# Two causal attentions of an eight-stage fp32 kernel: loads of later head groups issued from ScalarE one a unit, and a third weight buffer with a second accumulator

## The chip, the core and the metric

The kernel runs on one core of one Trainium2 chip. The core has TensorE (PE, matmuls; PEld in the profile is its weight load), VectorE (DVE), ScalarE (ACT), GpSimd (POOL) and SyncE (SP), which work side by side and wait for one another by semaphores. Each engine takes its own instructions in order. The metric is the device time of one execution in microseconds (us).

## What is computed

The reference passes `x`, 2048 rows of 128, through eight residual layers: RWKV, a mixture of experts, rotary attention, the mixture again, full attention, a second expert layer, latent attention, and that expert layer again. The change touches the two causal attentions:

```
q = apply_rope(q); k = apply_rope(k)                 # rotary: 16 heads of 8
scores = einsum('bhqd,bhkd->bhqk', q, k) / sqrt(8)
attn = softmax(where(causal, scores, -inf))
x = x + einsum('bhqk,bhkd->bhqd', attn, v) @ W_out.T

k = k_lat @ wk_up; v = v_lat @ wv_up                 # latent: 8 heads, 2 groups, rank 32
probs = softmax(where(causal, q @ k * 128**-0.5, min))
x = x + (probs @ v) @ wo
```

All is fp32 to the outside. Scores are made from operands that are split into three bf16 parts and stacked in the contraction rows.

## The kernel before

The whole program is one list of stages. `CausalHeads` (L1084) is used twice. Heads are worked four at a time, a "quad": four quads in the rotary stage, two in the latent one. A quad's 2048 queries are cut into four chunks `c` of 512 columns; a chunk has `4*(c+1)` key tiles, and one key tile of one chunk for four heads is a **unit**. The rotary stage goes through the chunks quad by quad (units 0 to 159, chunk (g,c) of quad g; quads begin at units 0, 40, 80 and 120), the latent stage alternates its quads (80 units; chunks begin at units 0, 4, 8, 16, 24, 36, 48 and 64).

In a unit PE makes the scores of two head pairs (`pe_scores`), ACT turns each pair into exponentials in a buffer `PT` (L1433), and one unit later PE multiplies them into bank 4 (`pe_weighted`, L1391). `PT` has two buffers, so the exponentials of unit u wait until unit u-2 has been used. At a chunk's end ACT copies bank 4 into `O` (L1442).

Between these, `make_plan` (L1197) lays out "ring items" in three PSUM banks that PE fills and DVE empties in order:

- `max`: part of the row maxima of a coming chunk. PE L1320 makes scores, DVE L1555 reduces them. After a chunk's last one DVE runs five small operations (L1564 to L1571) that make the negated maximum in three bf16 parts
- `turn`: PE transposes those parts (L1331), DVE copies them (L1577), and SP sends them by four DMAs into rows of `Q` (`max_row_dmas`, L1702)
- `sum`: the softmax denominators, broadcast; DVE then makes `On`, the normalised output (L1590 rotary, L1587 latent)
- `out`: PE projects `On` (L1349), DVE adds it to `X` (L1596)

The **rotary** stage gets its denominators as a ninth output row: SP moves them out of `O` into `sums` (L1736), DVE inverts them (L1533), SP moves them back (L1739), and PE broadcasts them (L1344). These two "relays" stand in the plan two and four units behind the end of the chunk, `sum` and `out` six and seven. DVE waits for the relay's DMA in its own order. Quad 0's stacked operands `Q` and `K` are loaded chunk by chunk (`load_early`). Those of quads 1 to 3 are loaded by SP in `sync`, with eight DMAs (`load_stacks`, L1626; three for `Q`, five for `K`, 2.3 MB in all), right behind the maximum rows of chunk (g,1). `Q` and `K` have two slots, so for g of 1 or more SP waits first until all units of quad g-1 are done. In SP's list this stands just ahead of the relay `sums` of quad g-1's last chunk.

The **latent** stage adds its exponentials up over the key tiles: for every unit POOL adds three heads and DVE one head of `PT` to `acc` (`add_weights`; L1475 copies at a chunk's first unit, L1477 adds at the others). There is one `acc`. The first unit of a chunk therefore waits, on both engines, until PE has read the last chunk's sums (L1340, one item in the tail of the second unit behind the chunk's end). `out` follows one unit behind `sum`. `PT` lies in the memory of `w0` and `w0b`, `acc` in `pbelow`, which are free by then; the trace shows these names.

POOL's other work is `Perturb.gpsimd` (L577 to L597), a search in 31 rounds for the second expert layer, that runs beside the rotary and the following stages.

Of the kernel before, what the change touches and what calls it, by code (L numbers as in the profile page):

```python
# [1083 lines left out]
class CausalHeads(Stage):  # L1084
# [76 lines left out]
    def alloc(self, ctx):  # L1161
# [5 lines left out]
        self.acc = self.homes[2] if self.summed else None  # L1167
# [10 lines left out]
        if self.homes:  # L1178
            self.PT = self.homes[0:2]
        else:  # L1180
            with ExitStack() as c:
                pt = self.k.sb(self.name + "_PT", [P, 2, 4, CH], F32, c)
                self.PT = [pt[:, b, :, :] for b in range(2)]
        with ExitStack() as c:
            self.x = self.k.sb(self.name + "_x", [P, ns, CH], F32, c)
            if self.rotate:
                self.y = self.k.sb(self.name + "_y", [P, CH], F32, c)
                self.tab = self.k.sb(self.name + "_tab", [P, 2, T], F32, c)
# [10 lines left out]
    def make_plan(self):  # L1199
# [31 lines left out]
        for n, (g, c) in enumerate(self.order):  # L1231
            end = self.starts[n + 1] - 1
            if self.summed:
                steps[end + 2].append(("sum", g, c))
                steps[end + 3].append(("out", g, c))
            else:
                relays.append((end + 2, "sums", g, c))
                relays.append((end + 4, "reciprocals", g, c))
                steps[end + 6].append(("sum", g, c))
                steps[end + 7].append(("out", g, c))  # L1240
# [66 lines left out]
    def pe_item(self, pe, item, bank):  # L1307
# [25 lines left out]
        if kind == "sum":  # L1333
            _, g, c = item
            n = self.chunk(g, c)
            if self.summed:
                pe.wait_ge(self.added[0], self.first_unit(n + 1))
                pe.wait_ge(self.added[1], self.first_unit(n + 1))
                for j in range(4):
                    ins = pe.matmul(k.PS[32 * j:32 * j + 32, bank, :], k.ones_col, self.acc[:, j, :],  # L1340
                                    start=True, stop=True)
# [37 lines left out]
    def pe_weighted(self, pe, u):  # L1379
# [9 lines left out]
        for j in range(4):  # L1389
            v = self.V[:, kj, (4 * g + j) if self.vheads > 4 else g, :]  # L1390
            ins = pe.matmul(k.PS[32 * j:32 * j + self.vcols, 4, q0:CH], v, self.PT[u % 2][:, j, q0:CH],  # L1391
# [4 lines left out]
    def scalar(self, s):  # L1396
# [26 lines left out]
        for u in range(total + 1):  # L1423
            if u < total:
                _, _, _, q0 = self.unit(u)
                if u >= 2:
                    s.wait_ge(self.weighted, u - 1)
                    if self.summed:
                        s.wait_ge(self.added[0], u - 1)
                        s.wait_ge(self.added[1], u - 1)  # L1430
                for p in range(2):
                    s.wait_ge(self.scores[p], u + 1)
                    s.activation(self.PT[u % 2][:, 2 * p:2 * p + 2, q0:CH], k.PS[:, 2 * p:2 * p + 2, q0:CH],  # L1433
                                 ACT.Exp, scale=self.scale).then_inc(self.exps[p], 1)
            if u:
# [26 lines left out]
    def add_weights(self, eng, u, who, heads):  # L1462
# [3 lines left out]
        if kj == 0 and n:  # L1466
            b, uses = self.ring_bank(self.ring_items().index(("sum",) + self.order[n - 1]))
# [5 lines left out]
        new, acc = self.PT[u % 2][:, heads, q0:CH], self.acc[:, heads, q0:CH]  # L1473
# [139 lines left out]
    def load_stacks(self, sp, g, cols, planes, done):  # L1613

        d = P // self.heads
        for operand, heads, (src, h), blocks in ((self.Q, 4, self.q_source(g), self.blocks[0]),
                                                 (self.K, self.kheads, self.k_source(g), self.blocks[1])):
            for block in blocks:
                for m, row, first, parts in self.parts_of(*block):
                    if m not in planes:  # L1620
                        continue
# [83 lines left out]
    def sync(self, sp):  # L1705
# [12 lines left out]
        for u, item in self.plan:  # L1718
            if item[0] == "turn":
# [7 lines left out]
                if c == 1 and self.early < len(self.order) and g + 1 < self.NQ:  # L1727
                    if g:
                        sp.wait_ge(self.weighted, self.starts[self.index[g, 0]])
                    self.load_stacks(sp, g + 1, slice(0, T), range(self.NP), self.stacked[(g + 1) % 2])  # L1730
# [259 lines left out]
def build(nc, d, upto=8, start=0):  # L1990
    with ExitStack() as ctx:
# [79 lines left out]
        def latent_attention():  # L2071
# [8 lines left out]
                            homes=[k.w0[:, :, :].rearrange("p (j e) h -> p j (e h)", j=4),  # L2080
                                   k.w0b[:, :, :, :].rearrange("p (j e) m d -> p j (e m d)", j=4),
                                   perturb.below[:, :, :, :].rearrange("p w s n -> p (w s) n")])
# [66 lines left out]
```

## Time and profile before

| | us |
|---|---|
| median of 3 runs (1888.04 to 1889.11) | 1888.36 |
| the profiled execution | 1890.95 |
| its span, from first to last instruction | 1888.7 |
| PE busy in the span | 1593.5 (84%) |
| DVE busy | 1159.4 (61%) |
| POOL busy | 818.2 (43%) |
| ACT busy | 787.2 (42%) |

The profiled execution took 2.6 us more than the median run, and 2.25 us of it lie outside its span. Times in the rows are us from the span's start. In a timeline row the first two numbers are start and duration, and the square brackets give how long the engine was idle before and what ended the idle time. Operations of one kind in a row are merged (x8). SPq and ACTq are DMA issues.

### The profile page before, as it was taken

The page shows a single profiled execution, that of the slowest core. Times are in us where ns is not written, and L with a number is a line of the kernel's source. Part 1 is how long each engine was busy: PE and PEld are TensorE (multiplying, and loading weights), DVE is VectorE, ACT ScalarE, POOL GpSimd, SP SyncE. Part 2 cuts the span into 40 slices and gives each one's busy share as a digit, 9 for nine tenths or more (in the row PEclk, how much of TensorE's full clock was granted, in tenths as well). Part 3 has the DMA queues.
Part 4 walks back from the last instruction along what each step waited for, and adds up shares of the span by engine and source line. Part 5 has one row for each costly group of instructions (what it writes and reads, how often), then busy time and mean ns, then how long its engine had stood idle before and what let it go on. Part 6 is the DMA issues. An engine that isn't in the chain of part 4 may idle for free. (4 is left out here: it accounts for less than half of the span.)

```text
span 1888.7 us, 25915 instructions
## 1 busy us (share of the span) xinstructions
PE 1593.5 (84%) x8863; PEld 804.5 (43%) x8863; DVE 1159.4 (61%) x2315; ACT 787.2 (42%) x1031; POOL 818.2 (43%) x987
## 2 busy tenths in 40 slices
PE   4766699769996996899979978998978889898779
PEld 2222466423332332333246655775644333333256
DVE  5887633499785785788343343334268888876551
ACT  2222233353553563565743333444442333444533
POOL 1224655455545463645455456000003456667900
PEclk8788699877998998999979999998988898988979
DMA  4000000143003002000000000000033000000000
GB/s 142 1 0 0 1 1 0 45 117 52 1 4 50 1 16 38 2 2 2 2 1 1 0 0 0 0 0 1 1 120 108 22 22 1 1 1 1 1 1 23
DMA packets 39122, 36.88 MB, mean 20 GB/s; under 512 B 10190, under 2 KB 36271, under 8 KB 38898
## 3 DMA queue, kind: packets, MB, share of 16 engines
q1 hardware_dynamic: 38842, 35.56, 7.9%
q8 instruction: 61, 1.00, 0.2%
q14 instruction: 35, 0.29, 0.1%
q10 hardware_dynamic: 120, 0.02, 0.0%
q0 software_dynamic: 64, 0.00, 0.0%
HBM read 26.10 MB, written 8.91 MB: 19 GB/s over the span
## 5 line engine op out<-in xcount | busy, mean ns | idle before, releaser
L1555 DVE TENSOR_REDUCE sb_rope_mp<-PS 128x1 f32<-128x512 f32 (+3 forms) x560 | 345.5, 669 | 70.3 <-PE PS L1324 32.9
L1433 ACT ACTIVATE sb_rope_PT<-PS 128x1024 f32<-128x1024 f32 (+3 forms) x320 | 273.3, 895 | 220.1 <-PE PS L1372 119.3
L1320 PE MATMUL PS<-sb_rope_K,sb_rope_Q 96*128 96x512 bf16 (+3 forms) x640 | 214.7, 375 | 43.7 <-DVE sb_rope_mp L1555 33.0
L1000 DVE SCALAR_TENSOR_TENSOR sb_X<-PS,sb_gates,sb_X 128x128 f32 (+1 forms) x320 | 90.1, 345 | 238.8 <-PE PS L948 238.6
L581 POOL TENSOR_SCALAR sb_pbelow<-sb_pa,sb_ptrial 128x512 f32<-128x512 f32 x124 | 196.2, 1593 | 6.4
L1555 DVE TENSOR_REDUCE sb_latent_mp<-PS 128x1 f32<-128x512 f32 (+2 forms) x280 | 174.9, 667 | 29.5 <-PE PS L1320 22.5
L588 POOL TENSOR_TENSOR sb_pbelow<-sb_pbelow 128x1024 f32<-128x1024 f32 (+1 forms) x248 | 181.8, 733 | 19.6
L936 PE MATMUL PS<-sb_HT,sb_w 128*128 (+1 forms) x384 | 182.5, 612 | 3.6 <-DVE sb_seed L519 1.9
L1372 PE MATMUL PS<-sb_rope_Q,sb_rope_K 99*128 99x512 bf16 (+3 forms) x640 | 181.5, 355 | 1.6 <-ACT sb_rope_PT L1433 0.9
L1372 PE MATMUL PS<-sb_latent_Q,sb_latent_K 96*128 96x512 bf16 (+7 forms) x640 | 160.0, 371 | 8.2 <-ACT sb_w L1433 4.7
L977 ACT ACTIVATE sb_moe_hidden<-PS,sb_vec 128x512 f32<-128x512 f32 x128 | 87.8, 687 | 159.7 <-PE PS L936 155.4
L1391 PE MATMUL PS<-sb_rope_PT,sb_rope_V 128*9 128x512 f32 (+3 forms) x1280 | 150.7, 543 | 0.1
L1320 PEld LDWEIGHTS PS<-sb_rope_K,sb_rope_Q 96*128 96x128 bf16 x640 | 60.0, 100 | 200.2 <-issue 88.1
L1475 POOL COPY sb_pbelow<-sb_w 128x1536 f32<-128x1536 f32 x8 | 13.2, 1655 | 293.7 <-ACT sb_w L1433 241.3
L1477 POOL TENSOR_TENSOR sb_pbelow<-sb_pbelow,sb_w0b 128x1536 f32<-128x1536 f32 (+2 forms) x40 | 118.0, 2949 | 45.9 <-ACT sb_w0b L1433 44.1
L948 PE MATMUL PS<-sb_w0b,sb_moe_hidden 128*128 128x128 f32 x1024 | 131.3, 281 | 0.0
L1320 PE MATMUL PS<-sb_latent_K,sb_latent_Q 96*128 96x512 bf16 (+3 forms) x320 | 105.6, 377 | 25.1 <-DVE sb_latent_rec L1585 11.9
L948 PEld LDWEIGHTS PS<-sb_w0b,sb_moe_hidden 128*128 128x128 f32 x1024 | 119.1, 191 | 14.5 <-issue 14.5
L1433 ACT ACTIVATE sb_w<-PS 128x1024 f32<-128x1024 f32 (+1 forms) x80 | 73.5, 938 | 109.6 <-PE PS L1376 40.4
L1477 POOL TENSOR_TENSOR sb_pbelow<-sb_pbelow,sb_w 128x1536 f32<-128x1536 f32 (+1 forms) x32 | 105.8, 3307 | 24.0 <-ACT sb_w L1433 22.2
L1433 ACT ACTIVATE sb_w0b<-PS 128x1024 f32<-128x1024 f32 (+2 forms) x80 | 67.3, 853 | 112.4 <-PE PS L1372 53.0
L594 POOL TENSOR_TENSOR sb_ptot<-sb_ptot,sb_prank 128x8 f32<-128x8 f32 x31 | 6.5, 211 | 225.2 <-issue 225.2
(296 smaller groups left out, 2552.7 us busy)
## 6 DMA issues: line engine op xcount, KB each, us to landing
sb_latent_Q<-latent_parts SPq DMA_DIRECT2D x48, 128.0 KB, 2.7
sb_rope_Q<-rope_parts SPq DMA_DIRECT2D x9, 384.0 KB
rope_parts<-sb_rope_parts SPq DMA_DIRECT2D x24, 128.0 KB, 2.4
latent_parts<-sb_latent_parts SPq DMA_DIRECT2D x12, 256.0 KB, 2.6
sb_rope_tab<-in_rotation SPq DMA_DIRECT2D x1, 2048.0 KB, 8.5
sb_rope_K<-rope_parts SPq DMA_DIRECT2D x6, 256.0 KB
latent_parts<-sb_latent_parts SPq DMA_DIRECT2D x12, 128.0 KB, 2.5
sb_latent_K<-latent_parts SPq DMA_DIRECT2D x48, 32.0 KB, 2.2
```

Source lines behind the costliest of these rows:

```text
L581: ch.mark(g.tensor_scalar(self.below[:, w, s, :], self.a[:, w, :], tr[:, 2 * w + s:2 * w + s + 1], None, ALU.is_lt))
L588: ch(g.tensor_tensor(bl[:, :, 0:n], bl[:, :, 0:n], bl[:, :, n:2 * n], ALU.add))
L936: pe.matmul(k.bank(b), self.w1(e, m), x, start=True, stop=True).then_inc(self.hid[b], 1)
L948: ins = pe.matmul(k.PS[:, 4 + b, i * P:(i + 1) * P], self.g[:, b, m, i * P:(i + 1) * P], self.w2(e, m), start=False, stop=(m == M - 1), sk ...
L977: s.activation(self.g[:, e % 2, m, :], k.bank(b), self.func, bias=self.b1(e, m)) \
L1000: ins = v.scalar_tensor_tensor(xi, k.PS[:, 4 + b:5 + b, i * P:(i + 1) * P], gate, xi, ALU.mult, ALU.add)
L1320: ins = pe.matmul(k.PS[:, bank, at:at + w], self.Q[0:self.rows, g % 2, j, 0, q0:q0 + P], self.K[0:self.rows, g % 2, j % self.kheads, 0, kc ...
L1372: ins = pe.matmul(k.PS[:, j, q0:CH], self.K[0:r, g % 2, j % self.kheads, m, kj * P:(kj + 1) * P], self.Q[0:r, g % 2, j, m, c * CH + q0:(c ...
L1391: ins = pe.matmul(k.PS[32 * j:32 * j + self.vcols, 4, q0:CH], v, self.PT[u % 2][:, j, q0:CH], start=(kj == 0), stop=(kj == last))
L1433: s.activation(self.PT[u % 2][:, 2 * p:2 * p + 2, q0:CH], k.PS[:, 2 * p:2 * p + 2, q0:CH], ACT.Exp, scale=self.scale).then_inc(self.exps[p ...
L1477: eng.tensor_tensor(acc, acc, new, ALU.add).then_inc(self.added[who], 1)
L1555: v.tensor_reduce(self.mp[:, n % 2, kc, heads[0]:heads[-1] + 1, i], k.PS[:, bank, 0:len(heads) * w].rearrange("p (h k) -> p h k", h=len(he ...
```

## The change

1. **Rotary, loads.** SP no longer loads the stacks of quads 1 to 3. ACT does it, from its own DMA queue, in the eight units of chunk (g,1): behind the exponentials of each unit it issues one of the eight DMAs (`load_quad`). At the first of them it waits for the units of quad g-1 or, for g=0, for the written constants and the stored parts.
2. **Latent, accumulators.** There are two `acc`, by parity of the chunk, the second in the memory of `H`. The first unit of a chunk waits for the sums of the chunk before the last, not of the last.
3. **Latent, buffers.** `PT` has a third buffer, in the memory of `HT` from column 1 on. The exponentials of unit u wait for unit u-3.
4. **Latent, output.** `out` stands two units behind `sum` in the plan, not one.

```diff
             if self.summed:
                 steps[end + 2].append(("sum", g, c))
-                steps[end + 3].append(("out", g, c))
+                steps[end + 4].append(("out", g, c))
...
-                if u >= 2:
-                    s.wait_ge(self.weighted, u - 1)
+                if u >= self.B:
+                    s.wait_ge(self.weighted, u - self.B + 1)
                     if self.summed:
-                        s.wait_ge(self.added[0], u - 1)
-                        s.wait_ge(self.added[1], u - 1)
+                        s.wait_ge(self.added[0], u - self.B + 1)
+                        s.wait_ge(self.added[1], u - self.B + 1)
                 for p in range(2):
                     s.wait_ge(self.scores[p], u + 1)
-                    s.activation(self.PT[u % 2][:, 2 * p:2 * p + 2, q0:CH], k.PS[:, 2 * p:2 * p + 2, q0:CH],
+                    s.activation(self.PT[u % self.B][:, 2 * p:2 * p + 2, q0:CH], k.PS[:, 2 * p:2 * p + 2, q0:CH],
                                  ACT.Exp, scale=self.scale).then_inc(self.exps[p], 1)
+                self.load_quad(s, u)
...
-        if kj == 0 and n:
-            b, uses = self.ring_bank(self.ring_items().index(("sum",) + self.order[n - 1]))
+        if kj == 0 and n >= 2:
+            b, uses = self.ring_bank(self.ring_items().index(("sum",) + self.order[n - 2]))
             eng.wait_ge(self.ring_full[b], uses + 1)
...
-        new, acc = self.PT[u % 2][:, heads, q0:CH], self.acc[:, heads, q0:CH]
+        new, acc = self.PT[u % self.B][:, heads, q0:CH], self.acc[n % 2][:, heads, q0:CH]
...
+    def load_quad(self, s, u):
+
+        g, c, kj, _ = self.unit(u)
+        if self.early == len(self.order) or g + 1 == self.NQ or c != 1:
+            return
+        if kj == 0:
+            if g:
+                s.wait_ge(self.weighted, self.starts[self.index[g, 0]])
+            else:
+                s.wait_ge(self.constants, self.constants0 + self.n_constants)
+                s.wait_ge(self.stored_lo, self.lo_done(NC - 1))
+                s.wait_ge(self.stored_hi, self.hi_done(NC - 1))
+        if kj < self.stack_dmas:
+            self.load_stacks(s, g + 1, slice(0, T), range(self.NP), self.stacked[(g + 1) % 2], [kj])
...
-                if c == 1 and self.early < len(self.order) and g + 1 < self.NQ:
-                    if g:
-                        sp.wait_ge(self.weighted, self.starts[self.index[g, 0]])
-                    self.load_stacks(sp, g + 1, slice(0, T), range(self.NP), self.stacked[(g + 1) % 2])
...
-                            homes=[k.w0[:, :, :].rearrange("p (j e) h -> p j (e h)", j=4),
-                                   k.w0b[:, :, :, :].rearrange("p (j e) m d -> p j (e m d)", j=4),
-                                   perturb.below[:, :, :, :].rearrange("p w s n -> p (w s) n")])
+                            homes=[[k.w0[:, :, :].rearrange("p (j e) h -> p j (e h)", j=4),
+                                    k.w0b[:, :, :, :].rearrange("p (j e) m d -> p j (e m d)", j=4),
+                                    k.HT[:, 1:1 + T].rearrange("p (j t) -> p j t", j=4)],
+                                   [perturb.below[:, :, :, :].rearrange("p w s n -> p (w s) n"),
+                                    k.H[:, :, :].rearrange("p (j n) d -> p j (n d)", j=4)]])
```

## Rows read from the trace of the kernel before

**Rows 1.** The page's first part: busy time of each engine, share, instructions.

```profile
PE 1593.5 (84%) x8863; PEld 804.5 (43%) x8863; DVE 1159.4 (61%) x2315; ACT 787.2 (42%) x1031; POOL 818.2 (43%) x987
```

**Rows 2.** Windows: span; busy PE, PEld, DVE, ACT, POOL; granted clock, DMA share, GB/s.

```profile
443.00:957.00 514.00, 452.20 (x3128) 173.19 (x3127) 363.35 (x647) 281.87 (x337) 264.91 (x441) 0.94 0.10 14
...
1430.00:1802.00 372.00, 317.10 (x1911) 124.43 (x1909) 292.55 (x405) 145.95 (x169) 237.00 (x80) 0.90 0.04 12
```

**Rows 3.** Timeline around quad 2's load, from 566 to 589 us.

```profile
566.16 2.18 SPq L1626 DMA_DIRECT2D sb_rope_K<-rope_parts  x5
...
568.38 0.60 SPq L1736 DMA_DIRECT2D sb_rope_sums<-sb_rope_O  x1
...
587.64 0.25 DVE L1533 RECIPROCAL sb_rope_rec<-sb_rope_sums 128x16 f32<-128x16 f32 x1 [15.34 <-DMA sb_rope_sums<-sb_rope_O]
...
588.50 0.61 PE L1320 MATMUL PS<-sb_rope_K,sb_rope_Q 96*128 96x512 bf16 x1 [14.90 <-DVE sb_rope_mp L1555]
```

**Rows 4.** Timelines around quad 3's load.

```profile
706.93 0.60 SPq L1736 DMA_DIRECT2D sb_rope_sums<-sb_rope_O  x1
...
726.56 0.25 DVE L1533 RECIPROCAL sb_rope_rec<-sb_rope_sums 128x16 f32<-128x16 f32 x1 [15.53 <-DMA sb_rope_sums<-sb_rope_O]
```

**Rows 5.** Windows just behind the two loads; columns as in rows 2.

```profile
588.00:604.00 16.00, 14.67 (x72) 4.79 (x73) 11.96 (x24) 6.31 (x7) 2.10 (x8) 0.77 0.01 2
...
726.50:742.00 15.50, 13.30 (x70) 4.53 (x70) 13.63 (x24) 6.30 (x7) 12.39 (x19) 0.83 0.01 2
```

**Rows 6.** Timelines at the rotary stage's start: what DMA issues take on either queue.

```profile
416.57 3.67 ACTq L1702 DMA_DIRECT2D sb_rope_Q<-sb_rope_negT  x4
...
433.82 3.16 SPq L1702 DMA_DIRECT2D sb_rope_Q<-sb_rope_negT  x4
```

**Rows 7.** SP's timeline: the relay's two DMAs, chunks (0,1) and (3,3).

```profile
481.81 0.58 SPq L1736 DMA_DIRECT2D sb_rope_sums<-sb_rope_O  x1
489.37 0.54 SPq L1739 DMA_DIRECT2D sb_rope_O<-sb_rope_rec  x1
...
952.81 0.55 SPq L1736 DMA_DIRECT2D sb_rope_sums<-sb_rope_O  x1
954.94 0.53 SPq L1739 DMA_DIRECT2D sb_rope_O<-sb_rope_rec  x1
```

**Rows 8.** Waits in the rotary stage: who for whom, us in total, times, longest.

```profile
ACT sb_rope_PT L1433 <- PE PS L1372: 119.3, 94, 6.6
...
PE PS L1331 <- DVE sb_rope_negp L1571: 22.5, 12, 4.0
```

**Rows 9.** Timeline of one chunk border of the latent stage (unit 16).

```profile
1511.45 1.06 PE L1340 MATMUL PS<-sb_pbelow,sb_cst 128*32 128x512 f32 x8
...
1512.59 0.43 DVE L1475 COPY sb_pbelow<-sb_w 128x512 f32<-128x512 f32 x1 [2.01 <-PE PS L1340]
...
1513.86 3.35 DVE L1585 RECIPROCAL sb_latent_rec<-PS 128x512 f32<-128x512 f32 x1
...
1517.26 0.61 PE L1320 MATMUL PS<-sb_latent_K,sb_latent_Q 96*128 96x512 bf16 x1 [2.00 <-DVE sb_latent_rec L1585]
...
1517.92 3.77 POOL L1477 TENSOR_TENSOR sb_pbelow<-sb_pbelow,sb_w 128x1536 f32<-128x1536 f32 x1
...
1519.98 2.27 DVE L1477 TENSOR_TENSOR sb_pbelow<-sb_pbelow,sb_w0b 128x512 f32<-128x512 f32 x1
```

**Rows 10.** Sum over windows of 15 to 21 us at the six borders before the last.

```profile
sum 113.00, PE 96.30 PEld 37.16 DVE 97.74 ACT 33.49 POOL 59.61; mean PE 16.05 PEld 6.19 DVE 16.29 ACT 5.58 POOL 9.94
```

**Rows 11.** POOL's timeline at the last border (unit 64).

```profile
1735.16 3.42 POOL L1477 TENSOR_TENSOR sb_pbelow<-sb_pbelow,sb_w0b 128x1536 f32<-128x1536 f32 x1 [0.65 <-ACT sb_w0b L1433]
1744.25 3.44 POOL L1477 TENSOR_TENSOR sb_pbelow<-sb_pbelow,sb_w 128x1536 f32<-128x1536 f32 x1 [5.67 <-ACT sb_w L1433]
1748.47 3.94 POOL L1477 TENSOR_TENSOR sb_pbelow<-sb_pbelow,sb_w0b 128x1536 f32<-128x1536 f32 x1 [0.78 <-ACT sb_w0b L1433]
```

**Rows 12.** Window of the rest of the last chunk; columns as in rows 2.

```profile
1748.00:1793.00 45.00, 33.87 (x220) 10.87 (x216) 26.62 (x14) 22.39 (x27) 43.59 (x13) 0.97 0.00 1
```

More of the change, by code:

```diff
@@ L1166, in alloc @@
         self.V = sb("V", [P, NT, self.vheads, self.vcols])
-        self.acc = self.homes[2] if self.summed else None
+        self.acc = self.homes[1] if self.homes else None
         self.mp = sb("mp", [P, 2, NC, 4, TPC])
@@ L1178, in alloc @@
         if self.homes:
-            self.PT = self.homes[0:2]
+            self.PT = self.homes[0]
+            self.B = len(self.PT)
         else:
@@ L1183, in alloc @@
                 self.PT = [pt[:, b, :, :] for b in range(2)]
+                self.B = 2
         with ExitStack() as c:
@@ L1339, in pe_item @@
                 for j in range(4):
-                    ins = pe.matmul(k.PS[32 * j:32 * j + 32, bank, :], k.ones_col, self.acc[:, j, :],
+                    ins = pe.matmul(k.PS[32 * j:32 * j + 32, bank, :], k.ones_col, self.acc[n % 2][:, j, :],
                                     start=True, stop=True)
@@ L1390, in pe_weighted @@
             v = self.V[:, kj, (4 * g + j) if self.vheads > 4 else g, :]
-            ins = pe.matmul(k.PS[32 * j:32 * j + self.vcols, 4, q0:CH], v, self.PT[u % 2][:, j, q0:CH],
+            ins = pe.matmul(k.PS[32 * j:32 * j + self.vcols, 4, q0:CH], v, self.PT[u % self.B][:, j, q0:CH],
                             start=(kj == 0), stop=(kj == last))
@@ L1611, in parts_of, with load_stacks @@
         return [(m, row + 32 * p, first + p, 1) for p in range(parts)]
-    def load_stacks(self, sp, g, cols, planes, done):
-        d = P // self.heads
+    def load_quad(self, s, u):
[11 more added lines that the diff above has]
+            self.load_stacks(s, g + 1, slice(0, T), range(self.NP), self.stacked[(g + 1) % 2], [kj])
+    def load_stacks(self, sp, g, cols, planes, done, only=None):
+        d, made = P // self.heads, 0
         for operand, heads, (src, h), blocks in ((self.Q, 4, self.q_source(g), self.blocks[0]),
@@ L1619, in load_stacks @@
                 for m, row, first, parts in self.parts_of(*block):
-                    if m not in planes:
+                    made += 1
+                    if m not in planes or (only and made - 1 not in only):
                         continue
```

## The prediction

> **What bounds the kernel now.** I read the page's first part, then windows by stage, then in the two stages that the change touches the waits, and at the longest waits the timeline. The page says that PE is busy 84% of the span and no other engine over 61% [rows 1]. That is a mean over eight stages, so it doesn't tell what this change is worth. The windows do: the rotary units last 514 us with PE busy 452, the latent ones 372 us with PE busy 317 and a mean granted clock of 0.90 [rows 2]. PE bounds both stages, except where something stops it, and those places are what an edit off PE can give back. Outside these two stages nothing changes.
>
> In the rotary stage the timeline shows one kind of large stop. SP has issued quad 2's eight loads, and the relay `sums` of chunk (0,3) is issued right behind them at 568.38. DVE, in order, reaches the reciprocal and sits idle for 15.34 us until that small transfer lands. The ring then stands full, PE is idle 14.90 us, and ACT with it [rows 3]. At quad 3's load the same follows: issued at 706.93, DVE idle 15.53 us [rows 4]. Quad 1's load comes ahead of the first unit and costs no such stop. In the latent stage each chunk border has its pattern: DVE idle 2.01 us for PE's sums, then a reciprocal of 3.35 us, which holds a ring bank, then PE idle 2.00 us for it [rows 9]. In the last chunk POOL is the bound instead: busy 43.59 of 45 us [rows 12].
>
> **Rotary, what is removed.** The relay no longer stands behind the loads. With an empty queue the relay goes from issue through reciprocal to the second issue in 2.13 us [rows 7]; at 566 or so DVE would have its sums at about 568.5, and it came for them at 587.64 - 15.34 = 572.3 [rows 3]. So both stops go entirely: 15.34 + 15.53 = 30.9 us, and since all engines stood still in them, nothing else fills the place. Behind each stop PE ran at a mean clock of 0.77 for 16 us and 0.83 for 15.5 us [rows 5], so up to 3.7 + 2.6 = 6.3 us more. I take 4, since the second window holds another short stop of its own.
>
> **Rotary, what is added.** ACT issues 24 DMAs. On SP the five `K` loads take 2.18 us, 0.44 each [rows 3]; four issues of maximum rows took 3.67 us on ACT and 3.16 on SP [rows 6], so a load's issue on ACT is about 0.44 x 3.67 / 3.16 = 0.51 us, 24 of them 12. They stand behind a unit's exponentials, ahead of the wait for the next unit's scores. ACT waits there: 94 times and 119.3 us in the stage [rows 8], 1.27 each. That covers 0.51, so I take 0; if the cover is gone it is 12. What is queued behind the issue is the next unit's exponentials and, at a chunk's end, the copy of bank 4; PE waits for both. The new waits at the first unit are for things long done (units before the last one, stores before the first): 0. Not below 0, since ACT issued none before.
>
> The loads are wanted at the next quad's first `max` items, units 23, 62 and 102 by the plan, and the last is issued in unit 11, 51 or 91. So eleven units lie between, over 30 us against 19.3 us for a whole load (568.38 to 587.64 [rows 3]): 0. But now the load moves while units run, and three relays (0,0), (1,0) and (2,0) fall in it. No row shows a small transfer beside another queue's load. Lower end: as with an empty queue, 2.1 us. Upper end: as behind everything, 19.3. The relay has 489.37 - 481.81 = 7.6 us until the reciprocal in the usual rhythm [rows 7]. One load in eight is 19.3 / 8 = 2.4 us; even behind two of them the relay lands in 2.1 + 4.8 = 6.9 us, so I take 0, and keep (19.3 - 7.6) x 3 = 35 us as the far end.
>
> The row shows only that one queue is served in order. The Trainium skill (DMA: Bandwidth & Descriptors, Issuing engines are not separate DMA queues) says that DMAs from any engine run on the same 16 DMA engines and interleave, and that another issuing engine only saves the sequencer's time to issue. That speaks against this part: by it alone the gain would be little more than the 3.3 us of issue per load; by the row it is 15.4 a load. The spread over eight units is what decides, and the rule has nothing against that.
>
> A shift of the rotary units also moves them against POOL's search. PE waited 22.5 us in 12 waits for DVE's small operations at `turn` [rows 8], some of which are stretched while POOL works. I take 0 and +-6 us.
>
> Rotary in sum: 30.9 + 4 = 35 us faster, from 20 to 43.
>
> **Latent, the last border.** POOL ends the add of unit 65 at 1738.6 and begins the next at 1744.25, idle 5.67 us for ACT, then 0.78 [rows 11]. The exponentials of unit 66 waited for DVE's copy of unit 64, which stands behind reciprocal and `On` in DVE's order, and the second pair waited for PE, which stood at `out` for `On`. With three buffers the copy is not asked for, and `out` comes a unit later. Then POOL goes on at once, and since it bounds what follows [rows 12], the stage ends 5.67 + 0.78 = 6.4 us sooner; I take 6.
>
> **Latent, the six others.** DVE's copy no longer waits for the sums (2.01 us), so the items behind it are done before they come and the reciprocal begins at the sums' end, 1512.5, not 1513.86: 1.3 us. PE's wait of 2.00 behind it shrinks by that, the exponentials no longer wait for POOL's copy, and PE's slow matmuls behind its idle time should go in part. The six windows have 113.0 - 96.3 = 16.7 us of PE idle, 2.8 a border [rows 10]. I take 2.5 a border with the clock, 15 us. Lower end 0: a later reciprocal's `On` may meet a POOL add. Upper end 5 a border: all idle time and as much again for the clock. Moving `out` costs no work; `H` and `HT` as homes change neither counts nor sizes, and only the chunk that begins at unit 8 has its first copy from `HT`. Latent in sum: 21 us, from 3 to 36.
>
> The rows show what limits it: DVE's add at 1519.98 took 2.27 us while POOL's ran from 1517.92 to 1521.69 [rows 9]. The Trainium skill (SBUF — State Buffer, SBUF: two separate sides) says that DVE and GpSimd share a port pair by an exclusive lock for a whole instruction. By that rule, the trace agrees: the add ended 0.56 us behind POOL's. By it a POOL that starts sooner is one that DVE meets more often, and the rule's own result is the slower rival below.
>
> **Rivals.**
> (A) *The relay crawls beside the loads.* For it: 2.3 MB are on their way in those units. Against: small transfer, 7.6 us of room. It costs up to 35 us of the 56: 1867. The stops would be three, at chunks (g,0).
> (B) *Latent gives only its last border or nothing*, because DVE's operations land behind POOL's adds: the gain is 35 + 0 to 6, 1847 to 1853. For it: the 2.27 us above. Against: POOL's adds are as many as before.
> (C) *Slower: DVE becomes the latent stage's bound.* With ACT free to run ahead, POOL starts each add before DVE comes to its own, and DVE waits for the whole of it, 3.42 us [rows 11], in each of the 64 units before the last chunk, 219 us. DVE has 372 - 292.6 = 79 us idle [rows 2], so 140 remain, less the 35 of the rotary part: 105 slower, 1993. It decides when the mean add grows by (79 + 35) / 64 = 1.8 us. Against: PE's own pace hardly lets ACT run ahead where `max` items fill the ring.
> (D) *ACT's issues have no cover and the relays crawl in part*: rotary gains 20, 1847.
>
> **How the numbers follow.** Forecast 35 + 21 = 56 us. In the profiled execution: span 1888.7 - 56 = 1832.7, with 2.25 outside 1835; the median run is 2.6 below, 1832.4. Say 1832. Chances: forecast with its own bounds (1814 to 1846) 0.68; (B) 0.15; (D) 0.07; (A) 0.05; (C) 0.03; no change 0.02. The range holds the forecast's spread, (B) and (D): 1815 to 1855. A difference of 0.2% (3.8 us) is about what a measurement of this kernel can tell from none; faster by more 0.95, within 0.02, slower 0.03.
>
> **What would show it.** Right: no DVE wait at L1533 of over 2 us near the quads' starts, the rotary units near 479 us instead of 514 in the windows; eight ACTq issues L1626 a quad; DVE's copy L1475 without a wait for L1340; POOL's copy under 1 us behind ACT's exponentials; POOL without a gap over 1 us behind unit 65; ACT no longer released by L1475. Wrong: L1533 released by DMA at chunks (0,0), (1,0), (2,0); ACT idle time released by PE falling by less than the issues; DVE adds L1477 of over 2 us in most units; latent units still 372 us.

## The result, and the profile after

The changed kernel takes 1856.18 us (median of 3 runs, 1855.55 to 1856.32) where the kernel before took 1888.36: a ratio of 0.983, 95% interval 0.981 to 0.985. It is faster, by 32 us and not by the 56 forecast, and 1856 lies 1.2 us above the range. The profiled execution took 1856.32 us, its span 1854.2.

The table splits it. "Rotary units" runs from the first exponential to the issue of the last chunk's `sums` relay, "latent units" from the first exponential to the end of POOL's last add; the four parts and the constant rest make up the span.

| us | before | after | gained | forecast |
|---|---|---|---|---|
| up to the first rotary exponential | 443.7 | 439.1 | 4.5 | 0 |
| rotary units | 509.2 | 479.1 | 30.1 | 35 |
| moe2, full attention, ffn1, latent projections | 478.0 | 482.2 | -4.2 | 0 |
| latent units | 362.2 | 358.0 | 4.2 | 21 |

First the windows of the changed kernel, with the columns of [rows 2]: the rotary and the latent stage, and POOL's last chunk, which answers to [rows 12].

```profile
439.00:918.00 479.00, 452.63 (x3125) 174.41 (x3123) 360.62 (x645) 280.11 (x336) 249.36 (x415) 0.97 0.08 17
1400.00:1767.00 367.00, 310.50 (x1910) 123.03 (x1908) 310.75 (x405) 146.57 (x169) 220.96 (x80) 0.90 0.04 12
1715.90:1758.50 42.60, 32.53 (x213) 10.63 (x212) 39.08 (x13) 22.59 (x26) 41.59 (x13) 0.93 0.00 1
```

In the rotary stage PE is busy as long as before (452.6 against 452.2 us), though the units are 30 us shorter (the window of [rows 2] is 4.8 us longer than its units, this one is not). The mean granted clock rose from 0.94 to 0.97, but PE's busy time didn't fall. In the latent stage POOL is busy 16 us less and DVE 18 us more, with as many instructions on each: DVE's operations have become longer. In the last chunk POOL is the bound as before.

The timelines of SP, ACT and DVE in the changed kernel around quad 2's load, which answer to [rows 3]:

```profile
573.08 0.30 ACTq L1645 DMA_DIRECT2D sb_rope_Q<-rope_parts  x1
573.40 1.02 ACT L1435 ACTIVATE sb_rope_PT<-PS 128x1024 f32<-128x1024 f32 x1
574.93 0.55 SPq L1751 DMA_DIRECT2D sb_rope_sums<-sb_rope_O  x1
...
585.56 0.24 DVE L1536 RECIPROCAL sb_rope_rec<-sb_rope_sums 128x16 f32<-128x16 f32 x1
585.82 0.59 SPq L1754 DMA_DIRECT2D sb_rope_O<-sb_rope_rec  x1
```

The relay goes between two loads, and the reciprocal has no wait in brackets. Before it sat idle for 15.34 us. ACT's issue takes 0.30 us and ends before the next exponential; up to 800 us, behind the last load, no wait of DVE for this transfer is left (30.9 us before, in two). The waits for the stage's last two relays stay, 11.8 and 20.1 us. They are in every trace (9 to 12 and 20 us) and have nothing to do with the loads: these relays are issued late, and are read 2 us behind their issue.

One border of the latent stage, which answers to [rows 9], from the timeline of the changed kernel:

```profile
1487.81 3.36 DVE L1588 RECIPROCAL sb_latent_rec<-PS 128x512 f32<-128x512 f32 x1 [0.23 <-PE PS L1342]
1491.04 3.42 POOL L1480 TENSOR_TENSOR sb_H<-sb_H,sb_w 128x1536 f32<-128x1536 f32 x1 [1.92 <-ACT sb_w L1435]
1491.20 3.80 DVE L1590 TENSOR_TENSOR sb_latent_On<-sb_latent_O,sb_latent_rec 128x512 f32<-128x512 f32 x1
1494.92 1.14 DVE L1558 TENSOR_REDUCE sb_latent_mp<-PS 128x1 f32<-128x384 f32 x2
1495.53 0.61 PE L1322 MATMUL PS<-sb_latent_K,sb_latent_Q 96*128 96x512 bf16 x1 [3.91 <-DVE sb_latent_mp L1558]
1497.96 1.02 ACT L1435 ACTIVATE sb_w0b<-PS 128x1024 f32<-128x1024 f32 x1 [7.09 <-PE PS L1374]
1501.62 3.62 POOL L1480 TENSOR_TENSOR sb_H<-sb_H,sb_w0b 128x1536 f32<-128x1536 f32 x1 [7.17 <-ACT sb_w0b L1435]
```

The waits that the edit was to remove are gone: no 2.01 us for the sums, no 2.00 behind the reciprocal. In their place stands `On`. It begins 0.16 us behind POOL's add and ends 0.54 us behind it. The maxima queue behind it, PE finds its ring full for 3.91 us, ACT waits 7.09 us for PE and POOL 7.17 us for ACT. The same comes at five borders. `On` over the stage (shortest, median, longest in ns, from the view of that line):

```profile
L1590 DVE TENSOR_TENSOR sb_latent_On<-sb_latent_O,sb_latent_rec x8: 691/3290/3803, 1425.1 to 1763.9; 128x512 f32<-128x512 f32 x8
```

In the kernel before, `On` came when a POOL add was nearly over. The timelines of POOL and DVE at the border of [rows 9]:

```profile
1514.41 3.43 POOL L1477 TENSOR_TENSOR sb_pbelow<-sb_pbelow,sb_w0b 128x1536 f32<-128x1536 f32 x1
1517.24 1.15 DVE L1587 TENSOR_TENSOR sb_latent_On<-sb_latent_O,sb_latent_rec 128x512 f32<-128x512 f32 x1
```

It began 0.60 us before that add's end and ended 0.55 us behind it, and POOL's next add, begun meanwhile at 1517.92, took 3.77 us instead of 3.42. Its median over the stage was 0.89 us.

### The profile page after: what moved, and what is told of

It is laid out like the page before. It is cut to its first block, busy times and chain, and to the rows that moved or that the text cites. A ratio compares the mean times of both kernels' runs of the same rounds, so it can differ in the third digit from the quotient of the medians.

```text
span 1854.2 us, 25913 instructions
## 1 busy us (share of the span) xinstructions
PE 1591.2 (86%) x8863; PEld 808.5 (44%) x8863; DVE 1173.7 (63%) x2315; ACT 787.9 (42%) x1031; POOL 802.9 (43%) x987
## 4 chain that ended last, share of the span: by engine, by line
PE 67%; DVE 15%; issue 3%; ACT 3%; POOL 2%; DMA 0%; DVEq 0%; POOLq 0%; SPq 0%; ACTq 0%
PE PS L1374 11%; PE PS L948 10%; PE PS L1322 10%; PE PS L936 9%; PE PS L1393 9%; PE PS L1822 3%; PE PS L1840 3%; DVE sb_rope_mp L1558 3%; POOL sb_H L1480 2%; DVE sb_latent_mp L1558 2%; DVE sb_latent_rec L1588 1%; PE PS L1834 1%; PE PS L941 1%; PE PS L1032 1%; PE PS L1351 1%
## 5 line engine op out<-in xcount | busy, mean ns | idle before, releaser
L936 PEld LDWEIGHTS PS<-sb_HT,sb_w 128*128 128x128 f32 x384 | 71.0, 199 | 71.7 <-issue 68.2
L1478 POOL COPY sb_pbelow<-sb_w 128x1536 f32<-128x1536 f32 x3 | 4.4, 1464 | 225.9 <-ACT sb_w L1435 219.3
L836 POOL TENSOR_TENSOR sb_rw_kvj<-sb_rw_k,sb_rw_vj 128x512 f32<-128x512 f32 x32 | 43.9, 1378 | 131.2 <-ACT sb_rw_vj L819 92.1
L1374 PEld LDWEIGHTS PS<-sb_latent_Q,sb_latent_K 99*128 99x128 bf16 (+1 forms) x640 | 59.0, 103 | 82.5 <-issue 22.3
L593 POOL PARTITION_ALL_REDUCE sb_ptot<-sb_pcnt x31 | 13.2, 427 | 186.3 <-issue 186.3
```

What stands on the lines that cost most here:

```text
L936: pe.matmul(k.bank(b), self.w1(e, m), x, start=True, stop=True).then_inc(self.hid[b], 1)
L1374: ins = pe.matmul(k.PS[:, j, q0:CH], self.K[0:r, g % 2, j % self.kheads, m, kj * P:(kj + 1) * P], self.Q[0:r, g % 2, j, m, c * CH + q0:(c ...
```

## The experiments

Three chips carried them. There one kernel's runs spread by 0.5 to 1%, so each time is read against the kernel before on the same chip (medians 1891.1, 1893.9, 1887.0 and 1887.2 us in the four groups), and most verdicts rest on the length of the two stages in the trace. The latent units of the changed kernel were 358.0 to 358.1 us in all five traces with that code, whatever the chip.

| kernel | rotary units | latent units | median us | ratio to before, 95% |
|---|---|---|---|---|
| before | 509.2 | 362.2 | 1888.4 | |
| changed | 479.1 | 358.0 | 1856.2 | 0.981 to 0.985 |
| changed, once more | 478.0 | 358.1 | 1854.2 | 0.976 to 0.988 |
| rotary part alone | 472.5 | 367.6 | 1862.3 | 0.980 to 0.989 |
| latent part alone | 506.4 | 358.1 | 1881.9 | 0.993 to 0.999 |
| burst from ACT | 509.0 | 358.0 | 1884.6 | 0.994 to 0.999 |
| spread from SP | 478.5 | 358.0 | 1852.9 | 0.976 to 0.985 |
| POOL held | 465.8 | 350.6 | 1849.4 | 0.974 to 0.983 |
| reciprocal in PSUM | 479.2 | 342.3 | 1832.4 | 0.964 to 0.971 |
| same, one accumulator | 471.7 | 359.5 | 1858.2 | 0.981 to 0.991 |
| same, latent part of before | 480.7 | 368.4 | 1864.4 | 0.982 to 0.992 |
| `HT` from element 0 | 465.3 | 362.5 | 1854.6, one run | |
| `w0` 8, `w0b` 64 bytes on | 476.0 | 359.4 | 1856.2, one run | |
| `w0` 4, `w0b` 36 bytes on | 468.4 | 347.2 | 1844.1 | 0.973 to 0.981 |
| reciprocal in PSUM and 4, 36 on | 475.3 | 329.1 | 1830.4 | 0.966 to 0.976 |
| the same, once more | 463.8 | 329.2 | 1825.9 | 0.962 to 0.974 |
| and `neg` in PSUM | 460.8 | 324.7 | 1813.7 | 0.955 to 0.966 |

**The two halves.** Each half with the other as before.

> The rotary part alone (quads' stacks loaded from ScalarE's queue, one transfer a unit; latent stage as in the kernel before). Theory: the rotary part is worth the two removed stops, 30 us between first exponential and last sums of the changed kernel's trace (509.2 against 479.1 us), and nothing is given back later: 1888.4 - 30 = 1858 us, 1854 to 1862. Rival: the clock behind the missing stops and POOL's search, which now meets other stages, take part of it back: 1866 or more, and then the latent part must be worth over 10.

> The latent part alone (two accumulators, three PT buffers, out two units behind sum; rotary loads as before). Theory: of the 21 us forecast only the last border's 6.4 us arrive, since at the five borders before it DVE's On multiply now begins just behind POOL's add and waits for its end (2.6 to 3.1 us each): latent units 362 to 358 us, so 1888.4 - 4 = 1884 us, 1881 to 1887. Rival: latent gained its 15 to 21 us and the rotary part gave less than the units' 30: 1867 to 1873.

Both came within their ranges but for 0.3 us (1862.3, 1881.9). The ranges were counted from 1888.4, though, and the kernel before took 1891.1 on this chip: read as gains, the latent half gave 9 us where 1 to 7 was expected, of which its latent units show 4.1. The rotary half is worth 29 us by the medians, the latent half 9, with an interval of 2 to 13. What neither text said: with its code unchanged, the latent stage took 367.6 us in the first, not 362.2. In the chunk that begins at unit 48, which took 73.2 us and not 64.4, three of DVE's own adds had fallen into step behind POOL's. The timelines of POOL and DVE in that kernel:

```profile
1647.41 3.42 POOL L1480 TENSOR_TENSOR sb_pbelow<-sb_pbelow,sb_w 128x1536 f32<-128x1536 f32 x1 [2.83 <-ACT sb_w L1435]
1647.45 3.93 DVE L1480 TENSOR_TENSOR sb_pbelow<-sb_pbelow,sb_w0b 128x512 f32<-128x512 f32 x1
```

An add of 0.67 us on its own takes 3.93 when it begins 0.04 us behind POOL's. So even the old stage isn't fixed to better than 5 us. Which engine comes first by some hundredths seems to decide it; what brings that about was not tried.

**Is it the queue or the spreading?** The first kernel issues all eight loads from ACT at once, the second one a unit from SP.

```diff
-        if kj < self.stack_dmas:
-            self.load_stacks(s, g + 1, slice(0, T), range(self.NP), self.stacked[(g + 1) % 2], [kj])
+        if kj == 0:
+            self.load_stacks(s, g + 1, slice(0, T), range(self.NP), self.stacked[(g + 1) % 2])
```

> The changed kernel, but ScalarE issues all eight loads of a quad at once in chunk 1's first unit, not one a unit: another queue, no spreading. Theory (order of one queue made the stops): the relay, on SP's own queue, still goes in 2 to 3 us beside the eight loads, DVE's waits for the sums stay under 3 us, time as the changed kernel, 1856 (1853 to 1860). Rival (the transfers share the DMA engines whatever the queue, so spreading was what helped): the relay crawls for most of the load's 19 us, DVE waits 5 to 15 us in two or three chunks, 1866 to 1886.

In SP's function, where `load_quad` now waits for unit u's exponentials ahead of its load:

```diff
         for u, item in self.plan:
-            if item[0] == "turn":
+            if item == "weighted":
+                self.load_quad(sp, u)
+            elif item[0] == "turn":
```

> The changed kernel, but SP issues the loads, one a unit behind the unit's exponentials, in its order with the relays: spreading, same queue. Theory (order of one queue, by quantity): the relay stands behind at most one load of 2.4 us, for which it has 7.6 us of room, so no stop comes back: 1856 (1853 to 1860). Rival (a relay behind any load on its queue is stopped for long): stops of over 5 us at the first chunk of quads 0 to 2, 1866 or more.

The burst brought the stops back, 1884.6 us: its relay, on SP's own and empty queue, was issued at 455.84, and its reciprocal came 19 us later; at the two other loads it was 19.9. Its timelines of SP and DVE, then DVE's waits from 440 to 800 us (total, times, longest):

```profile
455.84 0.63 SPq L1751 DMA_DIRECT2D sb_rope_sums<-sb_rope_O  x1
...
474.89 0.25 DVE L1536 RECIPROCAL sb_rope_rec<-sb_rope_sums 128x16 f32<-128x16 f32 x1 [11.14 <-DMA sb_rope_sums<-sb_rope_O]
```

```profile
DVE sb_rope_rec L1536 <- DMA sb_rope_sums<-sb_rope_O: 33.3, 3, 11.9
```

Spread over units from SP, the loads cost nothing, 1852.9 us, rotary units 478.5 (from ACT 479.1 and 478.0). So the spreading is the whole gain, and the change of engine is worth nothing here. The Trainium skill (DMA: Bandwidth & Descriptors, Issuing engines are not separate DMA queues) says that transfers share the 16 DMA engines whoever issues them. By that rule, the burst's trace agrees, with its 11.14 us.

**Is `On` long because of POOL?** First POOL's add of each chunk's third unit is made to wait for the `On` of the chunk before:

```diff
+        if who == 0 and kj == 2 and n:
+            eng.wait_ge(self.normed, n)
```

> The changed kernel, and POOL's add of each chunk's third unit waits for the On of the chunk before. Theory: On (3.29 to 3.80 us at five borders, 0.69 alone) lasts long only because it begins 0.04 to 0.18 us behind POOL's add; with POOL held for under 1 us it takes 0.7, PE's stops of 3 to 4 us behind it go, and POOL comes no later for its next exponentials, for which it waits 6.5 to 7.6 us now: (3.80 + 3.80 + 3.41 + 3.29 + 3.29) - 5 x 0.69 = 14 us faster, 1842, between 1836 and 1848. Rival: On's length is its own (its operands, its place), or PE is late for another reason: 1856 to 1858, and PE's stops stay.

`On` took 0.69 us at all five borders, so its length was POOL's. The latent units fell by 7.4 us, not by 14; the median, 1849.4, is just outside. The timeline shows where the other half went:

```profile
1478.35 0.69 DVE L1592 TENSOR_TENSOR sb_latent_On<-sb_latent_O,sb_latent_rec 128x512 f32<-128x512 f32 x1
1479.50 3.42 POOL L1482 TENSOR_TENSOR sb_H<-sb_H,sb_w 128x1536 f32<-128x1536 f32 x1 [3.23 <-DVE sb_latent_On L1592]
1480.03 3.44 DVE L1482 TENSOR_TENSOR sb_H<-sb_H,sb_HT 128x512 f32<-128x512 f32 x1
1484.13 0.61 PE L1322 MATMUL PS<-sb_latent_K,sb_latent_Q 96*128 96x512 bf16 x1 [3.08 <-DVE sb_latent_mp L1560]
```

The held add starts after `On`, and DVE's own add, next but one in its order, meets it. PE stops for 3.08 us instead of 3.91. That part of my expectation was wrong: I had taken the collision for one of `On` alone, and DVE's adds meet it as well.

Then `On` is given an operand in PSUM, and POOL isn't held:

```diff
-                v.reciprocal(self.rec[:, :], k.bank(bank)).then_inc(free, 1)
-                v.wait_ge(free, uses + 1)
-                v.tensor_tensor(self.On[:, n % 2, :], self.O[:, n % 2, :], self.rec[:, :], ALU.mult) \
+                ch(v.reciprocal(k.bank(bank), k.bank(bank)))
+                v.tensor_tensor(self.On[:, n % 2, :], self.O[:, n % 2, :], k.bank(bank), ALU.mult) \
...
+                v.wait_ge(self.normed, n + 1)
+                v.sem_inc(free, 1)
```

> The changed kernel, and the reciprocal is written in place into its PSUM bank, so that On multiplies SBUF by PSUM; POOL is not held. Theory: what DVE shares with POOL is used only by operations whose operands all lie in SBUF (maxima, which read PSUM, took 0.68 us beside every add); then On takes 0.7 us beside POOL's add and the time is about that of the kernel with POOL held, 1842, 1836 to 1850, the ring bank being held 1 us longer a border. Rival: On waits for POOL's add wherever its second operand lies: then also the bank is held for the whole add, and it is 1856 to 1870.

```profile
1489.24 3.42 POOL L1480 TENSOR_TENSOR sb_H<-sb_H,sb_w 128x1536 f32<-128x1536 f32 x1 [1.92 <-ACT sb_w L1435]
1489.41 0.69 DVE L1589 TENSOR_TENSOR sb_latent_On<-sb_latent_O,PS 128x512 f32<-128x512 f32 x1
1490.24 1.16 DVE L1558 TENSOR_REDUCE sb_latent_mp<-PS 128x1 f32<-128x384 f32 x2
1491.31 1.90 DVE L1480 TENSOR_TENSOR sb_H<-sb_H,sb_HT 128x512 f32<-128x512 f32 x1
1493.87 0.39 PE L1322 MATMUL PS<-sb_latent_K,sb_latent_Q 96*128 96x512 bf16 x1 [1.53 <-DVE sb_latent_mp L1558]
```

`On` begins 0.17 us behind POOL's add, in the very place where it took 3.80, and takes 0.69. DVE's add comes when half of POOL's is over. Latent units 342.3 us, 15.7 less than the changed kernel, and 1832.4 (4 us below the range). The theory holds. The Trainium skill (SBUF — State Buffer, SBUF: two separate sides) says that the exclusive lock is met by a DVE operation with two SBUF inputs, against a GpSimd operation that reads SBUF, or by one in a 2-port performance mode. By that rule, the rows agree: 0.69 with one SBUF input, 3.80 with two.

**What is the latent part worth without the collision?** The in-place reciprocal with the latent stage of before, and with everything of the change but the second accumulator (`self.acc = [self.homes[1][0]] * 2`, and the first copy of a chunk waits for the sums again):

> Rotary part as changed, latent stage as in the kernel before, but with the reciprocal in place in PSUM. It asks what the latent part is worth once On no longer meets POOL. Theory: On was 0.9 to 1.5 us in the old latent stage, 2.7 at the last border, so the in-place form brings it only some 4 us; DVE's and POOL's waits for PE's sums and POOL's 5.7 us at the last border stay: latent units 358 to 364 us, against 342.3 with the latent part, and 1855 to 1862. Rival: the in-place reciprocal is what helped, the latent part is worth nothing: units 342 to 346.

> The kernel with the reciprocal in place, but one accumulator instead of two (three PT buffers and out two units behind sum stay). Theory: the second accumulator is what lets POOL and DVE begin a chunk without waiting for PE's sums; without it the waits of about 2 us a border come back at DVE and POOL, and since ACT has a third buffer they are passed on only in part: latent units 342.3 + 1 to 2 a border, 348 to 357, 1840 to 1848. Rival: the third buffer alone carries it: 342 to 344.

The first gave 368.4 us, so in these traces the latent part is worth 26 us once `On` is out of POOL's way. I had expected 358 to 364; the in-place form alone gains nothing on the old stage (367.6). In both of these traces the chunk of unit 48 has DVE's adds in step behind POOL's (here three of 3.73 to 3.93 us, from 1659.96 to 1672.26). Against 362.2, the old stage without that, the latent part would be worth 20. The second gave 359.5 us, beyond the 357 expected, and 1858.2: the second accumulator carries 17 of it. The wait for the sums is back in its waits:

```profile
POOL sb_pbelow L1478 <- PE PS L1342: 55.6, 7, 11.3
```

**The 2.90 us adds.** In the changed kernel POOL's adds from `HT` took 2.90 us at the least, those from `w0` and `w0b` 3.42. `HT` is used from its element 1. Three kernels move the buffers by a few bytes:

```diff
-                                    k.HT[:, 1:1 + T].rearrange("p (j t) -> p j t", j=4)],
+                                    k.HT[:, 0:T].rearrange("p (j t) -> p j t", j=4)],
```

and, with `w0b` likewise (2 and 8 elements in the second kernel, 1 and 1 in the third):

```diff
-        k.w0 = sb("w0", [P, 8, 256])
+        k.w0 = sb("w0", [P, 1 + 8 * 256])[:, 1:].rearrange("p (e h) -> p e h", e=8)
```

> The changed kernel with the third PT buffer in HT from its element 0, not 1, so 4 bytes lower. POOL's adds with HT took 2.90 us where those with w0 and w0b took 3.42. Theory (the offset of 4 bytes against the accumulator does it): all adds take 3.42 now, and the time is up to 8 us longer, since POOL's adds of the last chunk stand in the path: 1858 to 1864. Rival (the place of HT in SBUF does it): adds with HT stay at 2.90, same time.

> The changed kernel with w0 8 bytes and w0b 32 bytes further on, HT at 4 bytes as before. Theory: what counts is that operand and accumulator differ in the low bits of a pair of 4-byte elements: adds with w0 (8) and w0b (32) take 3.42 us, with HT 2.90. Rival: any distance does it: 2.90 with w0 too, or with both.

> The changed kernel with w0 and w0b laid 4 bytes further on, as HT's columns lie. Theory (the offset of 4 bytes): POOL's adds with all three buffers take 2.90 us; the last chunk, where POOL goes without idle time, has ten adds with w0 or w0b of up to 0.52 us less, 4 us, and DVE waits for shorter adds before: 1849, 1845 to 1853. Rival (place): adds with w0 and w0b stay at 3.42, 1856.

POOL's adds grouped by form (busy, mean ns, idle before), first from element 0 of `HT`, then the second kernel, then the third:

```profile
L1480 POOL TENSOR_TENSOR sb_pbelow<-sb_pbelow,sb_HT 128x1536 f32<-128x1536 f32 x8 | 28.9, 3609 | 14.5 <-ACT sb_HT L1435 14.4
```

```profile
L1480 POOL TENSOR_TENSOR sb_pbelow<-sb_pbelow,sb_w0b 128x1536 f32<-128x1536 f32 x8 | 28.3, 3543 | 14.0 <-ACT sb_w0b L1435 14.0
...
L1480 POOL TENSOR_TENSOR sb_pbelow<-sb_pbelow,sb_w 128x1536 f32<-128x1536 f32 x8 | 24.7, 3092 | 22.0 <-ACT sb_w L1435 22.0
```

```profile
L1480 POOL TENSOR_TENSOR sb_pbelow<-sb_pbelow,sb_w 128x1536 f32<-128x1536 f32 x8 | 24.7, 3090 | 23.0 <-ACT sb_w L1435 23.0
L1480 POOL TENSOR_TENSOR sb_pbelow<-sb_pbelow,sb_w0b 128x1536 f32<-128x1536 f32 x8 | 24.1, 3018 | 10.7 <-ACT sb_w0b L1435 10.7
```

The latent units fell by 10.8 us with both buffers shifted, more than the last chunk's 5, probably since a shorter add also blocks DVE for less; the time, 1844.1 us, is 1 us below the range. From element 0 they rose by 4.5. The time of that kernel stayed at 1854.6: its rotary units were 13.8 us shorter than the changed kernel's, and the stages between 9.3 longer (491.5).

**Both together.**

> The two edits together on the changed kernel: reciprocal in place in PSUM, and w0 and w0b 4 bytes further on. Alone they brought the latent units from 358.0 to 342.3 and to 347.2 us. Theory (both take from the same thing, DVE standing behind POOL's adds, and only the last chunk's ten adds of 0.5 us are the shift's own): latent units 337 us, 335 to 340, and the time 1827, 1820 to 1834. Rival (independent): 342.3 - 10.8 = 331.5 us, 1821. Other rival: a new rhythm of DVE and POOL takes it back, 342 or more.

> The kernel with both edits once more, beside the one with neg in PSUM on the same chip. Expected: latent units 329 us as before, rotary units anywhere from 465 to 481 by where the search falls, 1830.

Latent units 329.1 and 329.2, better than the sum of the parts (331.5) and than I expected; 1830.4 and 1825.9 us.

**Why the rotary units vary.** With the same rotary code (spread loads) they took from 463.8 to 480.7 us. The idea is that the length goes with what meets POOL's search. The four small operations behind a chunk's maxima (`negp`, both operands in SBUF) took, in the sum from 440 to 903 us, 12.2 and 13.3 us where the units were 465.3 and 465.8, and 20.1 to 21.6 where they were 478.0 to 480.7; the other traces lie between, but for 463.8 at 14.9. The last kernel puts `neg` in PSUM:

```diff
-                neg, part = self.neg[:, n % 2, :, :], self.negp[:, n % 2, :, :, :]
+                neg = k.PS[:, bank, 0:4 * TPC].rearrange("p (j i) -> p j i", j=4)
+                part = self.negp[:, n % 2, :, :, :]
...
+                v.wait_ge(self.maxima, n + 1)
+                v.sem_inc(free, 1)
```

The last two lines free the bank, now behind the five operations.

> The kernel with both edits (reciprocal in place, w0 and w0b shifted), and the negated maxima `neg` of each chunk in the PSUM bank of the chunk's last max item instead of SBUF, so that each of the five small operations behind a chunk's maxima has an operand in PSUM. Theory: the rotary units' length (465 to 481 us in ten traces with the same rotary code) goes with how many of these operations meet POOL's search, and an operand in PSUM keeps them out of it: each takes under 0.25 us in the mean (before up to 0.62), PE's wait for negp in the rotary units falls from 15 to 22 us to about 14, rotary units 463 to 468 us; in the latent units the casts of up to 2.9 us go as well, 329 to 322 to 327; in all 1820 to 1826 against 1830. Rival: their length is not POOL's, or the bank held about 1 us longer a chunk costs as much: rotary units stay between 470 and 480, same time.

> The changed kernel itself beside these two. Theory (the latent units have one rhythm, the rotary ones go with the search): latent units 358.0 us again, rotary units from 465 to 481, with DVE's casts behind the maxima long where the units are long; 1850 to 1860.

The casts in the rotary units (busy, mean ns), in the changed kernel run once more and in this one:

```profile
L1573 DVE CAST sb_rope_negp<-sb_rope_neg 128x16 bf16<-128x16 f32 x14 | 6.0, 426 | 0.5
L1571 DVE CAST sb_rope_negp<-sb_rope_neg 128x16 bf16<-128x16 f32 x14 | 4.7, 339 | 0.5
```

```profile
L1574 DVE CAST sb_rope_negp<-PS 128x16 bf16<-128x16 f32 x14 | 2.4, 174 | 0.5
L1576 DVE CAST sb_rope_negp<-PS 128x16 bf16<-128x16 f32 x14 | 2.4, 174 | 0.5
```

And PE's wait for the parts, in the same order (16.7 us in 11 waits in the kernel with both edits, once more, which differs from this one by `neg` alone):

```profile
PE PS L1333 <- DVE sb_rope_negp L1574: 20.4, 12, 2.4
```

```profile
PE PS L1333 <- DVE sb_rope_negp L1577: 10.0, 6, 1.9
```

Every one of them takes 0.17 to 0.18 us now, rotary units 460.8, latent units 324.7, and 1813.7 us: better than expected, 3.95% under the kernel before and the fastest of all. Its four runs lie within 2.7 us (1812.7 to 1815.5), where the control's, the kernel with both edits beside it, spread over 9.4. That fits the idea that much of the spread was POOL's search meeting these operations at a different point in each run; with four runs each it isn't shown. By the medians it is 12.2 us faster than its control; the two traces lie only 6.3 apart (spans 1819.7 and 1813.4), since the control's profiled run was one of its fast ones. Of these 6.3 us the latent units have 4.5. The rotary units have 3.0, and the stages between, beside which the search still runs, lost 3.6 again (488.9 us against 485.3). So what `neg` in PSUM is worth to the rotary units stays open.

## Why the prediction missed, step by step

The direction was right; 24 us are missing. The latent term has 16.8 of them (21 against 4.2), the rotary one 4.9 (35 against 30.1), and the rest is that I took 2.6 off the profiled time for the median, while the changed kernel's profiled run lay at its median.

- *Rotary, stops removed, 31 + 4.* Both stops are gone, and the units are 30.1 us shorter in the compared traces, which is the 31 alone. The 4 for the clock doesn't show in them, as PE's busy time is the same. Over the twelve other traces with spread loads and `neg` in SBUF the mean is 473 us, 35 under the 507.8 of the two with SP's burst (509.2, 506.4), so the sum may hold in the mean. The +-6 us for POOL's search was too small for what it does, 17 us between the shortest and the longest.
- *Rotary, why.* The step "the relay no longer stands behind the loads" named the wrong half. I took the 2.13 us of an empty queue, and read [rows 3] as showing one queue served in order; the burst shows that an empty queue beside a running load gives 19 as well. What I gave as a remark, that spreading over eight units decides, was the mechanism.
- *ACT's 24 issues, 0.* Right: 0.27 to 0.37 us each (I had 0.51), beside the running exponentials.
- *Relays beside loads, 0.* Right: no wait of DVE, though issue to second issue took 10.9 us at 574.93, not 7.6.
- *Latent, last border, 6.* Mis-sized a little. POOL's last chunk, first copy to last add, went from 59.96 us (1733.05 to 1793.01) to 55.07: 4.9 us. Its waits behind unit 64's copy went from 7.1 us in three (0.65, 5.67, 0.78) to 4.3 in two, and the rest of the gain is the faster adds from `HT`, which the forecast didn't have:

```profile
1706.62 2.90 POOL L1480 TENSOR_TENSOR sb_H<-sb_H,sb_HT 128x1536 f32<-128x1536 f32 x1 [1.77 <-ACT sb_HT L1435]
...
1715.92 3.94 POOL L1480 TENSOR_TENSOR sb_H<-sb_H,sb_w0b 128x1536 f32<-128x1536 f32 x1 [2.56 <-ACT sb_w0b L1435]
```

- *Latent, the six others, 15.* This is the step that failed: 302.3 us before (1430.77 to 1733.05), 302.95 after (1400.43 to 1703.38), nothing gained. The working ended at the reciprocal. What its sum left out was `On` behind it. [rows 9] show when POOL's adds start, but not `On`: in the old order it began when a POOL add was nearly over. With the edit POOL's copy and first add come earlier, and its next add starts as soon as its exponentials are there, 0.04 to 0.17 us ahead of `On` at five borders. With `On` out of the way (the reciprocal in PSUM) the latent units fell by 15.7 us, 13.4 of them before the last chunk, which is about the size of the term. In the chunk of unit 8 three of DVE's adds took over 3 us as well, 10 us for its four full ones against 4 before. The collision of `On` was written down as the lower end, and as rival (B), with a chance of 0.15 for what turned out to be the outcome. Against it I wrote that POOL's adds are as many as before. True, but a collision is a matter of when, not of how many.
- *Rival (B)* gave 1847 to 1853 and was right in its mechanism: the time was 1856 since the rotary units had 5 us less and the latent stage only 4.2. The range's upper end came from (B)'s 1853 and was cut 2 us above it, without the +-6 of the search around it. With that it would have held the time.
- *Rival (C)* didn't come: DVE has 310.8 us busy in the latent stage's 367. *(A)* neither, thanks to the spreading; the burst shows its price, three stops of 33.3 us in all and rotary units of 509.0 us against 479.1.
- *Outside the two stages, 0.* The first rotary exponential came 4.5 us sooner, 3.3 of it because 16 normalising operations took 5.18 us instead of 8.44, and the stages between lost 4.2. Over all the traces these stretches took 437.5 to 443.7 and 477.7 to 491.5 us, so neither is likely to be the edit's; I gave them no width.

Of the signs named: no relay wait, 479 us, ACT's issues, DVE's copy without a wait for the sums and POOL's copy right behind the exponentials came as written. ACT was released by a first copy once more, by DVE's (4.4 us); a gap of 2.56 us of POOL behind unit 65 stayed, and "DVE adds of over 2 us" was too narrow a sign, as it named the adds and not `On`.

## What to carry to other kernels

When an edit lets one engine start earlier, list what the other engines do at that very time, and look for the pair that shares something: here a removed wait of 2 us became a stop of 3 to 4 us on PE because two operations began 0.2 us apart. Where POOL works beside DVE, give each DVE operation that others wait for an operand in PSUM. A small transfer that others wait for is protected from a large load by cutting the load up in time, not by another queue.

## What the runs showed of the hardware

- A POOL add of two SBUF operands of 1536 f32 a partition takes at the least 3.42 us when the operands' addresses differ by a multiple of 64 bytes, and 2.90 when by 4, 8 or 36 bytes more: 15% for an unused element ahead of the buffer.
- A DVE multiply of 128x512 f32 took 3.80 us with two SBUF inputs, begun 0.16 us behind a POOL add of 3.42, and 0.69 in the same place with one of them in PSUM.
- A DVE cast of 16 elements a partition from SBUF to SBUF takes 0.17 us, and up to 3.00 beside a POOL add (in the latent stage before); from PSUM it stayed at 0.174 in the mean of 14 beside POOL's search.
- A relay of 8 KB on an idle queue took 19 us, to the reciprocal that waited for it, beside 2.3 MB of loads issued on another just before it.
